# Two score buffers, masks half a row ahead and packed adjacency in a two-layer graph kernel

## The chip, the cores and the metric

The kernel runs on one core of one Trainium2 chip. The metric is the time of one execution on the device in microseconds (us); for a program on one core that is the time of this core. TensorE does the matrix products and the transposes, ScalarE the exponentials and many copies out of PSUM, VectorE the masks, maxima and sums, GpSimd (POOL in the profile) elementwise work on SBUF, and SyncE's queue issues the loads and stores.

## The reference

Inputs are `x` (4096 x 128), a sparse 0/1 matrix `adj` (4096 x 4096, on average 4 ones in a row), two scalars and `weights` (128 x 128), all float32.

```python
deg = clip(adj.sum(axis=1), 1.0);  dis = deg ** (-0.5)
diffusion = (dis[:, None] * adj * dis[None, :]) @ x - x
norms = maximum(norm(x, axis=-1), 1e-8)
sim  = x @ x.T / (norms[:, None] * norms[None, :])
attn = softmax(beta * sim * adj, axis=1)
L0   = diffusion + sigmoid(alpha) * (attn @ x - x)
x1   = layernorm(x + L0)
out  = layernorm(x1 + relu(adj @ (x1 @ weights)))
```

The softmax runs over all 4096 columns of a row: where `adj` is 0 the score is 0, not minus infinity. So the attention is dense, and each block of 128 rows needs 4096 cosines, 4096 exponentials and a product with all of `x`.

## The kernel before

The 4096 rows are 32 row blocks of 128. A row of `r` below is such a block. There are three stages, and inside each the order of every engine's instructions is written out by hand; engines meet only at semaphores (`wait_ge` on a count, `then_inc`).

**Attention stage.** A row is done in 8 steps `h`, each over 512 columns (one PSUM bank). The work on one row, in the order of its data:

1. `land_piece` (SyncE queue, L230) loads a quarter of the row of `adj`, 512 KB, into one of two landing buffers `land`. `cast` (ScalarE, L369) makes bytes of it in `adj_bytes[q]`, with another power of two for each quarter, and sums degrees. `pack` (GpSimd, L287 to L293) adds the four quarters' bytes into one quarter as many words, `packed`. `turn_adj` (TensorE, L838) transposes these into the bank `ps_at`, and `store_adj` (VectorE, L581) unpacks them with a shift and a mask, four operations a row, into `adjT`, which keeps the whole transposed adjacency in SBUF.
2. `cosines` (TensorE, L853): three matmuls (float16 high and low parts) give 128 x 512 cosines in one of two banks `ps_s`. They wait until the mask two groups earlier has read the bank.
3. `mask` (VectorE, L593) multiplies them by the adjacency bytes, writes the buffer `scores` and takes the maximum of the piece. There is one `scores` of 4096 columns. So `mask` of row r+1, step h, waits for `e_turned`: the transposes of row r, step h, have read the same place.
4. `row_max` (VectorE, L602 and L604), behind the last mask, gives the row's maximum. `exps` (ScalarE, L401) are four pieces of 1024 columns in place, with their sums.
5. `turn_e` (TensorE, L864): four transposes of 128 x 128 into one of four banks `ps_e`. `e_high` (ScalarE, L408) and `e_low` (VectorE, L608) copy them as float16 high and low parts to `eT_parts`, four deep.
6. `attend` (TensorE, L877 and L879): four pairs of matmuls add the step's part of the attention to the one accumulator bank `ps_acc`. It runs `LAG = 3` steps behind `turn_e`.
7. `attn_add` (VectorE, L615 and L618), after all eight `attend` of a row, scales `ps_acc` by 1 / sum and adds it to `u`.

Two waits tie this together at the accumulator:

```python
# TensorE, attend(r, h)
pe.wait_ge(e_lo, r * H + (h + 1))
if h == 0 and not start:
    pe.wait_ge(attn_read, r)             # attn_add of rows 0 .. r-1 done
# VectorE, attn_add(r)
dve.wait_ge(attn_part, r * H + H)        # all attend of row r done
```

TensorE's step of row r is: `turn_e(r, h)`; at h = 2 `turn_adj(r)`; then `attend(r, h - 3)`, or at h = 1 `attend(r-1, 7)`; then `cosines(r+1, h+1)` for h = 1 to 6. After step 7 come `attend(r, 5)`, `attend(r, 6)`, each with a cosine group of row r+2. VectorE's step is: at h = 2 `attn_add(r-1)`; `mask(r+1, h)`; at h = 7 `row_max(r+1)`; `e_low(r, h)`; from h = 4 `store_adj(r, h-4)`; from h = 5 a part of the row's sum. ScalarE does two `exps`, then `e_high(r, h)` with the other two `exps` behind h = 1 and 2 and a `cast` of row r+2 behind four others.

**Layer 0 sums.** For each row 32 matmuls (L918) add 8-bit adjacency tiles times `y` (two float16 parts of `x`, scaled by `dis`) in a bank of `ps_e`. `y` is made by GpSimd (L335, L339) and VectorE (`y_low`, L686) near the end of the attention stage, from a second load of `x` into free buffers (L247). The adjacency tiles of the first four rows are read straight from `adjT`; for the others `stage_block` (VectorE, L682) copies a row of `adjT` into one of two stage buffers. Behind the sums VectorE adds (L725, L728) and normalises; TensorE, ScalarE and VectorE make `x1 @ weights` four rows behind (L924, L929, L464, L756).

**Layer 1 sums.** The same with `x1 @ weights` instead of `y`, then relu, add, normalise (L735 to L750), and the store.

Of the kernel before, what the change touches and what calls it, by code (L numbers as in the profile page):

```python
# [26 lines left out]
ALU = mybir.AluOpType  # L27
# [23 lines left out]
def two_layer_gnn(nc, x, adj, alpha, beta, weights, out):  # L51
# [12 lines left out]
    with ExitStack() as ctx:  # L64
# [10 lines left out]
        adjT = sb("adjT", [P, R, B, P], U32)  # L75
        land = sb("land", [P, 2, CH], F32)
# [4 lines left out]
        scores = sb("scores", [P, N], F32)  # L81
# [3 lines left out]
        col = sb("col", [P, 29], F32)  # L85
        packed = sb("packed", [P, CH // K], U32)
# [5 lines left out]
        cmax = sb("cmax", [P, H], F32)  # L92
        csum = sb("csum", [P, C], F32)
# [6 lines left out]
        neg_max, total, r_total, gain = (c(n) for n in range(6, 10))  # L100
# [18 lines left out]
        land_full = [sem("land_full0"), sem("land_full1")]  # L119
        x_again = [sem(f"x_again{q}") for q in range(C)]  # L120
# [72 lines left out]
        x_again_at = ([land[:, q, :].rearrange("p (r d) -> p r d", d=D) for q in range(2)]  # L193
                      + [adj_bytes[:, q, :].bitcast(F32).rearrange("p (r d) -> p r d", d=D) for q in range(2)])
        y_parts = xn_parts[:, :, :].rearrange("p a (r d) -> p r a d", d=D)
        x1t = scores[:, 0:2 * P].rearrange("p (a d) -> p a d", d=P)
        x1_now = scores[:, 2 * P:6 * P].rearrange("p (a d) -> p a d", d=P)
        wts = scores[:, 6 * P:7 * P]
        summed = scores[:, 7 * P:9 * P].rearrange("p (a d) -> p a d", d=P)
# [6 lines left out]
        packed_f = packed[:, :].bitcast(F32)  # L206
        stage = [adj_bytes[:, q, :].bitcast(U32) for q in range(2)]
        stage8 = [adj_bytes[:, q, :].bitcast(F8).rearrange("p (b i k) -> p b i k", b=B, k=K) for q in range(2)]
        adjT8 = [adjT[:, r, :, :].rearrange("p b i -> p (b i)").bitcast(F8)
                 .rearrange("p (b i k) -> p b i k", b=B, k=K) for r in range(G)]  # L210
        adjT_rows = adjT[:, :, :, :].rearrange("p r b i -> p r (b i)")
# [8 lines left out]
        def _(sp):  # L220
            sp.dma_start(u_b[:, 0:2, :], x_v[:, 0:2, :]).then_inc(x_loaded[0], 16)
            sp.dma_start(alpha_c, alpha.rearrange("(a o) -> a o", o=1).to_broadcast([P, 1])).then_inc(small_loaded, 16)
            sp.dma_start(beta_c, beta.rearrange("(a o) -> a o", o=1).to_broadcast([P, 1])).then_inc(small_loaded, 16)
            for q in range(1, C):
                sp.dma_start(u_b[:, 2 * q:2 * q + 2, :], x_v[:, 2 * q:2 * q + 2, :]).then_inc(x_loaded[q], 16)
            sp.dma_start(wts_early, weights).then_inc(w_loaded, 16)

            def land_piece(b, k, i):

                sp.dma_start(land[:, i % 2, :], adj_v[b, k, :, i * CH:(i + 1) * CH]).then_inc(land_full[i % 2], 16)  # L230
# [779 lines left out]
```

## Time and profile before

| | before |
|---|---|
| median of 3 runs | 761.27 us (760.44 to 761.53) |
| span of the profiled execution, first to last instruction | 757.8 us |
| TensorE busy | 721.4 us (95% of the span) |
| VectorE busy | 572.1 us (75%) |
| ScalarE busy | 494.4 us (65%) |
| GpSimd busy | 128.7 us (17%) |
| read from HBM | 71.44 MB |
| attention stage ends (first matmul of layer 0) | 518.0 us |
| layer 0 sums end, layer 1 sums begin | 639.1 us |

The profiler takes one execution; for it the table gives the span on the engines, and the runs' times, taken without a profile, lie 3.5 us above that span in the median. A busy share is an average over stages with different limits, and a busy TensorE is not one at its peak: its matmuls overlap, so durations add up to more than the time they hold the engine. For work on TensorE the distance from start to start is the number to read. On VectorE too an operation's successor can start some 0.07 us before its recorded end.

### The profile page before, as it was taken

Reading aid. Unit: us, or ns where it says so; the run is one execution under the profiler, and the core shown is the slowest. Engines: PE = TensorE matmul, PEld = TensorE weight load, DVE = VectorE, ACT = ScalarE, POOL = GpSimd, SP = SyncE. Lnnn points to the kernel's source line nnn. Section 1 sums busy time; section 2 is a strip of 40 time slices with the busy share of each in tenths; the row PEclk is TensorE's granted clock in tenths of the full one; section 3 lists DMA queues with packets and bytes.
Section 4 is the critical chain, followed back from the end, with each engine's and each line's share of the span. In section 5 each row is a group of like instructions: output and inputs, shape, how many; then the busy total and the mean of one; then the engine's idle time right before and its main releaser. Section 6 shows DMA issues by size and latency. Waiting matters only on the chain. (4 is left out here: it accounts for less than half of the span.)

```text
span 757.8 us, 19379 instructions
## 1 busy us (share of the span) xinstructions
PE 721.4 (95%) x6163; PEld 578.5 (76%) x6163; DVE 572.1 (75%) x1644; ACT 494.4 (65%) x1001; POOL 128.7 (17%) x161
## 2 busy tenths in 40 slices
PE   6889989999999999999999999989999999999997
PEld 6567767777777777777777777768999998888886
DVE  4878878887888788878887888797566666465655
ACT  5888899889988998899889988982122223211111
POOL 2781112111211121112111211170000000000000
PEclk9999999999999999999999999999999999999999
DMA  5645543455445534553445345510000000000000
GB/s 177 189 139 143 159 132 124 127 152 160 115 129 151 160 114 131 150 159 115 130 150 159 115 131 149 169 51 5 1 0 0 0 0 0 12 17 14 28 14 28
DMA packets 22502, 73.81 MB, mean 97 GB/s; under 512 B 2640, under 2 KB 3152, under 8 KB 22480
## 3 DMA queue, kind: packets, MB, share of 16 engines
q1 hardware_dynamic: 22480, 73.54, 32.5%
q8 instruction: 11, 0.18, 0.1%
q14 instruction: 11, 0.09, 0.0%
HBM read 71.44 MB, written 2.10 MB: 97 GB/s over the span
## 5 line engine op out<-in xcount | busy, mean ns | idle before, releaser
L593 DVE CUSTOM_DVE_ANT_1 scores<-ps_s,adj_bytes 128x512 f32<-128x512 f32 x252 | 172.5, 685 | 72.7 <-PE ps_e L864 67.8
L853 PE MATMUL ps_s<-xn_parts,xn_signed 128*128 128x512 f16 x756 | 204.4, 380 | 1.7 <-DVE cmax L593 1.7
L877 PE MATMUL ps_acc<-x_parts,eT_parts 128*128 128x256 f16 x1024 | 192.8, 272 | 4.6 <-DVE u L618 2.0
L879 PE MATMUL ps_acc<-x_parts,eT_parts 128*128 128x128 f16 x1024 | 180.9, 219 | 0.0
L608 DVE SCALAR_TENSOR_TENSOR eT_parts<-ps_e,eT_parts 128x512 f16<-128x512 f32 x256 | 175.2, 685 | 3.7 <-ACT eT_parts L408 3.1
L864 PEld LDWEIGHTS ps_e<-ident,scores 128*128 128x128 f32 x1024 | 123.0, 141 | 69.7 <-issue 27.6
L408 ACT ACTIVATE eT_parts<-ps_e 128x512 f16<-128x512 f32 x256 | 147.0, 587 | 37.3 <-PE ps_e L864 36.6
L864 PE MATMUL ps_e<-ident,scores 128*128 128x128 f32 x1024 | 150.1, 274 | 18.4 <-ACT scores L401 18.4
L401 ACT ACTIVATE scores<-scores,col 128x1024 f32<-128x1024 f32 x128 | 157.6, 1231 | 1.1 <-DVE col L604 1.1
L369 ACT ACTIVATE adj_bytes<-land 128x1024 uint8<-128x1024 f32 x128 | 135.2, 1057 | 23.3 <-DMA land<-in_adj 22.7
L877 PEld LDWEIGHTS ps_acc<-x_parts,eT_parts 128*128 128x128 f16 x1024 | 100.0, 98 | 24.0 <-issue 9.6
L918 PE MATMUL ps_e<-xn_parts,adj_bytes 128*128 128x256 f16 x896 | 105.4, 273 | 0.0
L879 PEld LDWEIGHTS ps_acc<-x_parts,eT_parts 128*128 128x128 f16 x1024 | 100.1, 98 | 5.3
L918 PE MATMUL ps_e<-x_parts,adj_bytes 128*128 128x256 f16 x896 | 98.0, 273 | 0.0
L918 PEld LDWEIGHTS ps_e<-x_parts,adj_bytes 128*128 128x128 fp8e4 x896 | 87.7, 98 | 10.1
L918 PEld LDWEIGHTS ps_e<-xn_parts,adj_bytes 128*128 128x128 fp8e4 x896 | 87.7, 98 | 9.5
L853 PEld LDWEIGHTS ps_s<-xn_parts,xn_signed 128*128 128x128 f16 x756 | 60.2, 98 | 42.5 <-issue 2.1
L287 POOL TENSOR_TENSOR packed<-adj_bytes 128x256 uint32<-128x256 uint32 x32 | 23.3, 728 | 357.9 <-PE ps_at L838 357.9
L453 ACT ACTIVATE col<-mv,col 128x1 f32<-128x1 f32 x64 | 18.6, 291 | 97.7 <-DVE mv L721 97.7
L682 DVE COPY adj_bytes<-adjT 128x1024 uint32 (+1 forms) x56 | 38.8, 693 | 50.2 <-PE ps_e L918 50.2
L487 ACT ACTIVATE scores<-ps_e,col 128x128 f32<-128x128 f32 x32 | 11.8, 369 | 88.9 <-PE ps_e L918 88.9
L581 DVE TENSOR_SCALAR adjT<-ps_at 128x256 uint32 (+1 forms) x128 | 52.6, 413 | 0.0
(113 smaller groups left out, 570.1 us busy)
## 6 DMA issues: line engine op xcount, KB each, us to landing
land<-in_adj SPq DMA_DIRECT2D x128, 512.0 KB, 3.6
u<-in_x SPq DMA_DIRECT2D x4, 512.0 KB, 8.0
out<-u SPq DMA_DIRECT2D x7, 256.0 KB, 2.0
land<-in_x SPq DMA_DIRECT2D x2, 512.0 KB, 3.3
adj_bytes<-in_x SPq DMA_DIRECT2D x2, 512.0 KB, 3.8
out<-u SPq DMA_DIRECT2D x1, 192.0 KB, 1.9
eT_parts<-in_L_gnn_weights SPq DMA_DIRECT2D x1, 64.0 KB, 9.0
scores<-in_L_gnn_weights SPq DMA_DIRECT2D x1, 64.0 KB, 1.7
```

The costliest lines, as they stand in the source:

```text
L369: nc.scalar.activation(adj_bytes[:, q, i * CH:(i + 1) * CH], land[:, i % 2, :], ACT.Copy, scale=float(BYTE_ONE >> i), accum_out=deg[:, i, ...
L401: nc.scalar.activation(scores[:, i * CH:(i + 1) * CH], scores[:, i * CH:(i + 1) * CH], ACT.Exp, bias=neg_max, scale=abs_beta, accum_out=cs ...
L408: nc.scalar.activation(eT_parts[:, h % 4, 0, :], ps_e[:, h % 4, :], ACT.Copy, scale=E_SCALE).then_inc(e_hi, 1)
L581: nc.vector.tensor_scalar(adjT_rows[:, r, i * CH // K:(i + 1) * CH // K], ps_at[:, 0:CH // K].bitcast(U32), i, BYTE_ONE * 0x01010101, ALU. ...
L593: nc.vector.tensor_tensor_reduce(scores[:, o:o + BANK].rearrange("p (k q) -> p k q", k=K), score_bank(h, start).rearrange("p (k q) -> p k ...
L608: nc.vector.scalar_tensor_tensor(eT_parts[:, h % 4, 1, :], ps_e[:, h % 4, :], E_SCALE, eT_parts[:, h % 4, 0, :], ALU.mult, ALU.subtract).t ...
L682: nc.vector.tensor_copy(stage[q], adjT_rows[:, r, :]).then_inc(staged, 1)
L853: ins = nc.tensor.matmul(score_bank(h, start), xn_signed[:, q, part, :], xn_parts[:, other, o:o + BANK], start=(part == 0 and other == 0), ...
L864: ins = nc.tensor.transpose(ps_e[:, h % 4, n * P:(n + 1) * P], scores[:, t * P:(t + 1) * P], ident[:, :])
L877: nc.tensor.matmul(ps_acc[:, 0:2 * D], eT_parts[:, h % 4, 0, n * P:(n + 1) * P], x_parts[:, t, :], start=(t == 0), stop=(t == R - 1), skip ...
L879: ins = nc.tensor.matmul(ps_acc[:, 0:D], eT_parts[:, h % 4, 1, n * P:(n + 1) * P], x_parts[:, t, 0:D], start=False, stop=(t == R - 1), ski ...
L918: return nc.tensor.matmul(ps_e[:, n, 0:2 * D], lhs[:, b, :, k], y[t], start=(t == 0), stop=(t == R - 1))
```

## The change

- **Two score buffers.** `scores` becomes two buffers, one for even and one for odd rows, and `cmax`, `csum`, `neg_max` become two each. `mask` of row r waits for the transposes of row r-2 instead of r-1.
- **Masks and cosines half a row ahead.** In row r, steps 0 to 3 do cosine groups and masks 4 to 7 of row r+1, steps 4 to 7 do groups 0 to 3 of row r+2. `row_max(r+1)` comes in step 3. The prologue does four groups of row 1 instead of two.
- **TensorE's order.** In each step: `turn_e`, at h = 2 `turn_adj`, then `attend` (in steps 0, 1, 2 groups 5, 6, 7 of the previous row), then the cosines. Nothing is left behind step 7.
- **ScalarE's order.** `e_high` and a cast in steps 0 to 3, `e_high` and a piece of the next row's exponentials in steps 4 to 7. In the prologue all exponentials of row 0 and two casts come before the first `e_high`.
- **VectorE's order.** `attn_add(r-1)` moves to step 3. `y_low` moves to steps 4 to 7 of row 31.
- **Packed adjacency.** `store_adj` is one copy of the packed words to `packT`, a quarter of `adjT`'s size. The unpacking moves to `stage_block`: four shift-and-mask operations a row, for all rows of both layers, into one of four stage buffers. Those of rows 0 to 3 of layer 0 are done between the steps of row 31.
- **Buffers.** `land` has four quarters instead of two. `x` is kept in `x_keep`, so the second load of `x` goes. `packed` has two buffers.

```diff
-        adjT = sb("adjT", [P, R, B, P], U32)
-        land = sb("land", [P, 2, CH], F32)
+        packT = sb("packT", [P, R, CH // K], U32)
+        stage = sb("stage", [P, G, N // K], U32)
+        land = sb("land", [P, C, CH], F32)
+        x_keep = sb("x_keep", [P, R, D], F32)
-        scores = sb("scores", [P, N], F32)
+        scores = sb("scores", [P, 2, N], F32)
...
 # SyncE
-                        sp.wait_ge(cast_done, b * (K * C) + (k * C + i - 1))
+                        sp.wait_ge(cast_done, b * (K * C) + ((k - 1) * C + i + 1))
...
 # GpSimd
-                    pool.wait_ge(adj_turned, r)
+                    pool.wait_ge(adj_turned, r - 1)
...
             pool.wait_ge(dis_done, 1)
+            pool.wait_ge(s_done, R * H)
             for q in range(C):
-                pool.wait_ge(x_again[q], 16)
-                y_q = x_again_at[q]
+                y_q = x_keep[:, q * TC:(q + 1) * TC, :]
...
 # ScalarE
             def row(r, q, start=False):
-                casts = (4, 5, 6, 7) if start else (3, 4, 6, 7)
-                exps(r, 0)
-                exps(r, 1)
-                for h in range(H):
-                    if start and h == 2:
-                        cast(1, 1, 3, first=True)
+                for h in range(C):
                     e_high(r, h, start)
...
+                    cast(r + 2, q, h)
+                for h in range(C, H):
+                    e_high(r, h, start)
+                    exps(r + 1, 1 - q, h - C)
+
+            exps(0, 0, 0)
+            cast(1, 1, 2, first=True)
+            exps(0, 0, 1)
+            exps(0, 0, 2)
+            cast(1, 1, 3, first=True)
+            exps(0, 0, 3)
...
 # VectorE
+            def store_adj(r):
+
+                dve.wait_ge(adj_turned, r + 1)
+                nc.vector.tensor_copy(packT[:, r, :], ps_at[:, 0:CH // K].bitcast(U32)).then_inc(adj_stored, 1)
...
                 if not start:
-                    dve.wait_ge(e_turned, r * H + (h + 1 - H))
+                    dve.wait_ge(e_turned, r * H + (h + 1 - 2 * H))
...
-                    if h == 2 and not start:
+                    if h == 3 and not start:
                         if second:
                             dve.wait_ge(u_init, C)
                         attn_add(r - 1)
-                    mask(r + 1, 1 - q, h)
-                    if h == H - 1:
-                        row_max(r + 1)
+                    if h < C:
+                        mask(r + 1, 1 - q, h + C, start)
+                    elif not degrees:
+                        mask(r + 2, q, h - C)
+                    if h == C - 1:
+                        row_max(r + 1, 1 - q)
                     e_low(r, h)
-                    if h >= 4:
-                        store_adj(r, h - 4)
+                    if h == C:
+                        store_adj(r)
                     if h >= 5:
...
-                nc.vector.tensor_copy(stage[q], adjT_rows[:, r, :]).then_inc(staged, 1)
+            def stage_block(k, r, n):
+                for i in range(C):
+                    nc.vector.tensor_scalar(stage[:, n, i * CH // K:(i + 1) * CH // K], packT[:, r, :], i,
+                                            BYTE_ONE * 0x01010101, ALU.logical_shift_left,
+                                            ALU.bitwise_and).then_inc(staged, 1)
...
 # VectorE, row 31
             for h in range(H):
-                if h == 2:
+                if h == 3:
                     attn_add(R - 2)
...
                 e_low(R - 1, h)
...
+                if h < C:
+                    stage_block(h, h, h)
+                if h >= C:
+                    y_low(h - C)
+                if h == C:
+                    store_adj(R - 1)
...
 # VectorE, layers
-                if lag >= G and more:
-                    stage_block(r + 2, n % 2)
+                stage_block(r + G, ahead, n)
                 head0(r, n)
...
 # TensorE
                 for h in range(H):
-                    turn_e(r, h, start)
+                    turn_e(r, q, h, start)
                     if h == 2:
-                        turn_adj(r, start)
+                        turn_adj(r, q, start)
                     if h >= LAG:
                         attend(r, h - LAG, start)
-                    elif h == 1 and not start:
-                        attend(r - 1, H - 1)
-                    if left and 1 <= h < H - 1:
-                        cosines(r + 1, 1 - q, h + 1)
-                for h in range(H - LAG, H - 1):
-                    attend(r, h, start)
-                    if left > 1:
-                        cosines(r + 2, q, h - (H - LAG))
+                    elif not start:
+                        attend(r - 1, h + H - LAG, second)
+                    if h < C and left >= 1:
+                        cosines(r + 1, 1 - q, h + C)
+                    elif h >= C and left >= 2:
+                        cosines(r + 2, q, h - C)
...
-                pe.wait_ge(staged, r + (layer * (R - G) - G + 1))
+                pe.wait_ge(staged, r * C + (layer * R * C + C))
```

## Rows read from the trace of the kernel before

**Rows 1.** The page, busy time by engine: us (share of span) x instructions.

```profile
PE 721.4 (95%) x6163; PEld 578.5 (76%) x6163; DVE 572.1 (75%) x1644; ACT 494.4 (65%) x1001; POOL 128.7 (17%) x161
```

**Rows 2.** Busy time by stretch: us, engines, clock, DMA; rows 30-31, layer 0.

```profile
490.86:518.01 27.15, 23.60 (x222) 19.62 (x223) 25.14 (x58) 21.41 (x36) 15.69 (x11) 1.00 0.18 60
518.01:639.11 121.10, 121.10 (x1111) 109.50 (x1109) 77.19 (x247) 27.10 (x114) 0.00 (x0) 1.00 0.00 0
```

**Rows 3.** Timeline of TensorE, one row block: start, us, line, xcount [idle before].

```profile
218.13 1.09 PE L864 MATMUL ps_e<-ident,scores 128*128 128x128 f32 x8 [0.43 <-ACT scores L401]
...
221.10 0.82 PE L853 MATMUL ps_s<-xn_parts,xn_signed 128*128 128x512 f16 x3
221.75 0.60 PE L864 MATMUL ps_e<-ident,scores 128*128 128x128 f32 x4
222.43 0.27 PE L877 MATMUL ps_acc<-x_parts,eT_parts 128*128 128x256 f16 x1
...
223.09 0.81 PE L853 MATMUL ps_s<-xn_parts,xn_signed 128*128 128x512 f16 x3
...
233.28 0.98 PE L864 MATMUL ps_e<-ident,scores 128*128 128x128 f32 x7 [0.44 <-ACT scores L401]
```

**Rows 4.** Timeline of VectorE in the same row block.

```profile
219.03 0.69 DVE L593 CUSTOM_DVE_ANT_1 scores<-ps_s,adj_bytes 128x512 f32<-128x512 f32 x1 [2.17 <-PE ps_e L864]
...
220.35 0.68 DVE L593 CUSTOM_DVE_ANT_1 scores<-ps_s,adj_bytes 128x512 f32<-128x512 f32 x1
...
220.96 0.68 DVE L608 SCALAR_TENSOR_TENSOR eT_parts<-ps_e,eT_parts 128x512 f16<-128x512 f32 x1
221.56 0.34 DVE L615 SCALAR_TENSOR_TENSOR u<-ps_acc,col,u 128x128 f32 x1
221.93 0.35 DVE L618 SCALAR_TENSOR_TENSOR u<-ps_acc,col,u 128x128 f32 x1
```

**Rows 5.** Timeline of ScalarE in the same row block.

```profile
221.31 0.58 ACT L408 ACTIVATE eT_parts<-ps_e 128x512 f16<-128x512 f32 x1
221.79 1.24 ACT L401 ACTIVATE scores<-scores,col 128x1024 f32<-128x1024 f32 x1
...
223.02 0.58 ACT L408 ACTIVATE eT_parts<-ps_e 128x512 f16<-128x512 f32 x1
...
224.53 0.59 ACT L408 ACTIVATE eT_parts<-ps_e 128x512 f16<-128x512 f32 x1
```

**Rows 6.** Timeline of row 31, VectorE and then TensorE.

```profile
509.96 0.35 DVE L618 SCALAR_TENSOR_TENSOR u<-ps_acc,col,u 128x128 f32<-128x128 f32 x1
...
510.46 0.27 PE L877 MATMUL ps_acc<-x_parts,eT_parts 128*128 128x256 f16 x1 [0.91 <-DVE u L618]
```

**Rows 7.** Groups of instructions by line: busy us, mean ns, idle before.

```profile
L581 DVE TENSOR_SCALAR adjT<-ps_at 128x256 uint32 (+1 forms) x128 | 52.6, 413 | 0.0
L682 DVE COPY adj_bytes<-adjT 128x1024 uint32 (+1 forms) x56 | 38.8, 693 | 50.2 <-PE ps_e L918 50.2
...
L686 DVE TENSOR_TENSOR xn_parts<-land,xn_parts 128x1024 f16<-128x1024 f32 x2 | 3.4, 1684 | 0.0
```

**Rows 8.** Timeline between the layers, VectorE and then TensorE.

```profile
639.09 0.35 DVE L725 SCALAR_TENSOR_TENSOR u<-ps_e,dis_out,u 128x128 f32<-128x128 f32 x1 [1.12 <-PE ps_e L918]
...
641.51 0.49 PE L929 MATMUL ps_acc<-scores 128*128 128x128 f32 x2 [0.27 <-ACT scores L460]
```

**Rows 9.** Timelines of the start: ScalarE, then TensorE twice.

```profile
31.75 1.24 ACT L401 ACTIVATE scores<-scores,col 128x1024 f32<-128x1024 f32 x1 [0.31 <-DVE col L604]
...
13.93 3.62 PE L819 MATMUL ps_e<-ident,scores 128*128 128x128 f32 x16 [4.08 <-DVE scores L534]
...
49.83 1.09 PE L864 MATMUL ps_e<-ident,scores 128*128 128x128 f32 x8 [2.13 <-ACT scores L401]
```

**Rows 10.** Busy time by stretch around the two gaps; the clock is third from last.

```profile
12.00:20.00 8.00, 5.21 (x31) 4.87 (x32) 6.79 (x15) 6.61 (x27) 4.73 (x3) 0.79 0.38 124
...
45.00:53.00 8.00, 5.87 (x50) 4.15 (x48) 4.50 (x15) 7.12 (x13) 6.54 (x8) 1.00 0.59 190
```

More of the change, by code:

```diff
@@ L118, in two_layer_gnn @@
         w_loaded = sem("w_loaded")
[L119 to L120 removed]
+        land_full = [sem(f"land_full{i}") for i in range(C)]
         ident_zero = sem("ident_zero")
@@ L205, in two_layer_gnn @@
         words = [adj_bytes[:, q, :].bitcast(U32).rearrange("p (i w) -> p i w", i=C) for q in range(2)]
[L206 to L211, printed above, removed]
+        packed_f = [packed[:, q, :].bitcast(F32) for q in range(2)]
+        stage8 = [stage[:, n, :].bitcast(F8).rearrange("p (b i k) -> p b i k", b=B, k=K) for n in range(G)]
         def score_bank(h, start):
@@ L394, in _, with exps, e_high @@
             cast(1, 1, 1, first=True)
[L395 to L397 removed]
+            def exps(r, q, i):
                 if i == 0:
                     act.wait_ge(max_done, r + 1)
[L401 to L404 removed]
+                piece = scores[:, q, i * CH:(i + 1) * CH]
+                nc.scalar.activation(piece, piece, ACT.Exp, bias=neg_max[q], scale=abs_beta,
+                                     accum_out=csum[:, q, i:i + 1]).then_inc(exp_done, 1)
+            def e_high(r, h, start=False):
                 act.wait_ge(e_turned, r * H + (h + 1))
@@ L447, in _ @@
                 row(r + 1, 1)
-            late_row(R - 2, 0)
-            late_row(R - 1, 1)
+            e_high(R - 2, 0)
+            e_high(R - 2, 1)
+            e_high(R - 2, 2)
+            act.wait_ge(deg_done, 1)
+            nc.scalar.activation(dis[:, :], dis[:, :], ACT.Sqrt).then_inc(deg_root, 1)
+            e_high(R - 2, 3)
+            nc.scalar.activation(table_loads[1], eps_c, ACT.Exp)
+            for h in range(C, H):
+                e_high(R - 2, h)
+                exps(R - 1, 1, h - C)
+            for h in range(H):
+                e_high(R - 1, h)
+                if h == 0:
+                    nc.scalar.activation(table_loads[2], eps_c, ACT.Sqrt)
             def root(r, q, base):
@@ L648, in _ @@
                                          ALU.mult, ALU.mult))
+            for h in range(C):
+                mask(1, 1, h, start=True)
             def row(r, q, start=False, second=False, degrees=False):
@@ L904, in _ @@
                 cosines(0, 0, h, start=True)
-            cosines(1, 1, 0)
-            cosines(1, 1, 1)
+            for h in range(C):
+                cosines(1, 1, h)
             row(0, 0, start=True)
-            row(1, 1)
+            row(1, 1, second=True)
             with pe.Fori(2, R - 3, 2) as r:
@@ L913, in _ @@
             row(R - 1, 1, left=0)
-            attend(R - 1, H - 1)
+            for h in range(H - LAG, H):
+                attend(R - 1, h)
             def add_tile(n, lhs, t, y):
```

201 lines of the change are left out of this document (77 added, 124 removed).

## The prediction

> **What bounds the kernel now.** I read the page first: TensorE is busy in 95% of the span [rows 1], so I went on to the cut by stage and there to the timeline of one row block [rows 2, 3]. The attention stage, 32 row blocks one after the other, ends at 518 us, two thirds of the span. In the first of the two later stages (sums over the adjacency) TensorE is busy 121.10 of 121.10 us, and the change leaves those matmuls as they are. So what matters is the period of a row block: 15.15 us, from 218.13 to 233.28 in the timeline of one [rows 3].
>
> TensorE's own work in one block, from start-to-start distances in the same rows: four transposes are 0.60 us, of which the last takes 0.27, so 0.11 each, 32 of them 3.52 and the two of the adjacency 0.22; four pairs of attention matmuls 0.66 (222.43 to 223.09), eight times 5.28; a cosine group 0.65 (221.10 to 221.75), eight times 5.2. Sum 14.2 us. The other 0.95 us of the 15.15 is waiting. Most of it lies at the head of the block, where the transposes wait for the exponentials [rows 3]: with one score buffer the masks of the next row can only follow the transposes, so the row's maximum, and the exponentials behind it, come late. About 0.24 us of it is another wait, and it is the one this prediction turns on: `attend(r, 0)` starts at 222.43, though the transposes in front of it started at 221.75 and hold TensorE for 0.44. It waits until VectorE has taken the previous row's sum out of `ps_acc` (`attn_add`, L615 and L618): L618 starts at 221.93, lasts 0.35 and ends at 222.28, and the matmul follows 0.15 later [rows 3, 4]. In row 31 the same wait is plain: the matmul at 510.46 has stood 0.91 us for L618 [rows 6]. So before the change this wait is just about covered, with nothing to spare.
>
> **What the steady row loses.** With two score buffers and masks half a row ahead, the maximum of row r+1 is known at step 3 of row r. Its exponentials run in steps 4 to 7, ahead of the transposes that need them, so the wait at the head of the block goes. ScalarE's step with an exponential piece takes 1.71 us and one with a cast 1.51 (221.31, 223.02, 224.53) [rows 5], TensorE's step is 0.44 + 0.66 + 0.65 = 1.75. ScalarE needs 12.9 us in a block and fits under it, barely in the second half. Four landing buffers give each load almost a block to arrive. VectorE loses three of four unpacking operations of 0.33 a row. None of that is on the path any more, so by themselves these edits would bring the block to 14.2 us, 28 us less over the stage.
>
> **What the steady row gains.** `attn_add(r-1)` moves from step 2 to step 3 of VectorE's row. The last attention group of row r-1 moves from TensorE's step 1 to its step 2, and `attend(r, 0)` stays in step 3. Before, two cosine groups and two of transposes lay between the two; now one of each does. More than that: VectorE's step 2 is `mask(r+1, 6)`, then `e_low(r, 2)`, and `attn_add(r-1)` is queued behind both. `mask(r+1, 6)` needs the cosine group 6, which TensorE issues last in its own step 2. In the kernel before the mask of a step used the cosines of the step before. So the chain from the start of that cosine group is: group 0.82 (its x3 row at 221.10 [rows 3]); start of the mask 0.30 later; mask to `e_low` 0.61 (220.35 to 220.96); `e_low` 0.60 (to 221.56); L615 to L618 0.37; L618 0.35 [rows 4]; to the matmul 0.15 (509.96 + 0.35 to 510.46) [rows 6]. Sum 3.20 us. TensorE is ready for `attend(r, 0)` after 0.65 + 0.44 = 1.09. **Stall: 2.1 us in every block from row 1 on.** Queued behind it on TensorE is cosine group 7, and for that wait `mask(r+1, 7)`, the maximum and the exponentials, but these have a whole half block in hand: from the end of the stall ScalarE's four steps of 1.71 run beside four of 1.75 and are caught up at the next head. I find no second wait.
>
> The 0.30 is the least sure term. The trace has the mask waiting for transposes: those of step 0 end by 218.13 + 0.60, the mask starts at 219.03 [rows 4]. A wait for cosines is not in it. The bounds: 0.03, as L725 starts after its last matmul [rows 8], and 0.45, half as much again as the 0.30, since one more wait instruction stands behind the one that blocks. I take 0.30, the same instruction's own row. The stall is then between 1.85 and 2.25.
>
> The block becomes 14.2 + 2.1 = 16.3 us. Rows 1 to 29 took from 49.83 [rows 9] to 490.86, 441.0 us; they will take 29 x 16.31 = 473.0. **Plus 32** (24 to 36 over the bounds).
>
> **The ends.** *Start:* ScalarE begins the exponentials of row 0 at 31.75 [rows 9] and now does all four (1.23 each, 221.79 to 223.02) and two casts (1.51 less 0.48 for the `e_high`) before the first `e_high` [rows 5], to about 38.8. `attend(0, 0)` then starts near 40.1, and with 0.66 + 0.65 and four steps of 1.75 row 1 starts near 48.5, against 49.83, where TensorE had stood 2.13 us. Two cosine groups more and two attention groups less are done by then, which about cancel (1.30 against 1.32). **Minus 1.2** (0 to minus 2.4).
>
> *Rows 30 and 31* took 27.15 us to the first matmul of the next stage [rows 2]. Now, from the start of row 30: four steps 7.2 with the longer stall of this row 2.4, then 0.6 to the next `e_high` and 0.9 until the maximum is there (mask 7, then L602 and L604), four ScalarE steps with exponentials 6.8, and the first piece of row 31: 18.0. From there VectorE is the bound, because four new unpackings of four operations are put between the pieces of row 31: eight `e_low` 4.8, sixteen operations of 0.335 (0.413 less what overlaps) 5.4, three of the four `y_low` at 1.21 3.6, one copy 0.33, one `attn_add` 0.75, small ones 0.4: 15.3, then 0.8 for the last attention group. Sum 34.1, **plus 7.0**. `y_low` can be longer while GpSimd runs beside it; the mean of the two from `land` is 1.68 [rows 7], which makes 1.5 more, 2.8 if all are as its longest.
>
> The sixteen operations read SBUF, where L581 read PSUM; a copy of 1024 such elements from SBUF to SBUF takes 0.693, only 1.7 times what the 256 of L581 take [rows 7]. At that copy's rate an operation would take some 0.2: the lower bound, 2.2 less. I keep 0.335: same operation, same shape. The Trainium skill (VectorE: DVE Perf Modes, "The perf-mode tier table") lets a 32-bit `tensor_scalar` between SBUF tiles run at two elements a cycle and one from PSUM not. The copy's row agrees for a copy; by that rule the sum would be 2.2 us less here and 0.5 less below.
>
> *Later stages:* a row of the first has VectorE busy 77.19 / 32 = 2.4 of its 3.8 us [rows 2]; four operations (1.34) for one copy (0.61) make it 3.1, some 3.4 with the gaps between dependent ones, so it stays hidden behind TensorE; if that cover went, each 0.1 us over would cost 28 x 0.1 = 2.8. At the change of layers the last row's unpacking now stands in front of L725, which starts at 639.09 and from which the chain leads to the matmul at 641.51, where TensorE already stands 0.27 [rows 8]. **Plus 1.3** (0.8 to 1.4).
>
> Sum: 32.0 - 1.2 + 7.0 + 1.3 = +39.1. The span goes from 757.8 to 797; the median of the runs is 3.5 above that span: 761.3 + 39 = **800 us**.
>
> **The rivals.** *The wait does not bind (faster).* The accumulator wait stays as small as it is if `attn_add(r-1)` is through before TensorE wants `ps_acc`. That needs the chain of 3.20 us to be under 1.09; the sides change at a stall of 0.95, which makes the block 15.15 again. For it: 0.24 was all that it cost before. Against: row 31, where a VectorE busy with other work made it a wait of 0.91 [rows 6], and each of the chain's terms has a row. With no stall: 29 x 14.2 = 411.8, ends as above less 2.4: 737 us. Chance 4%; 1% for ending within 0.2%.
>
> *The clock falls.* Each block now has a gap of 2.1 us, row 30 one of 2.4. After a gap of 4.08 us sixteen transposes took 3.62, twice their pitch, with the granted clock at 0.79 over 12 to 20 us, a mean of its two levels 1.2 and 2.4 GHz; around the gap of 2.13 us before 49.83 it was 1.00 [rows 9, 10]. If each block lost as the start did, half of 3.6 us, that is 29 x 1.8 = 52 more: 852 us. Chance 5%. The Trainium skill (TensorE: Matmul & The Clock Gate, "Part 1: The HAM clock gate") has the clock throttled by default and released by activity, so it speaks against a schedule with holes; the start of this trace agrees, the 2.13 us gap bore no such cost.
>
> *Only the steady stall, cheap ends.* Rows 30 and 31 keep near their old time because unpacking runs at 0.2 and ScalarE sets the pace: 793. It is inside the forecast's range.
>
> **How the numbers follow.** The forecast has 90%. Its range: 800 less 8 (stall), 2.7 (unpacking), 1.2 (start) is 788; plus 4, 2.8 (`y_low`), 1.2 is 808. I add some 3 below and 2 above, as the ends were put together from many small terms: 785 to 810. About what a measurement can tell is 0.2%: faster 0.05, same 0.01, slower 0.94.
>
> **What would show it.** After the change: row blocks 16.3 us apart; TensorE waiting for L618 about 29 times 2.1 us; no wait for exponentials at the head of a block and none of ScalarE for landings; the mask waiting for cosines in each first half; VectorE without a gap through row 31; granted clock 1.00. A block of 14 to 15 us would make the prediction wrong, as would a wait of TensorE for L618 of under 1 us.

## The result and the profile after

The changed kernel takes 822.92 us in the median of 4 runs (822.49 to 825.49), the kernel before 760.97 (760.44 to 761.53) beside it: ratio 1.083, interval 1.081 to 1.085. The direction was forecast, the time was not: 800 was predicted, with 785 to 810 as its range. The profiled execution has a span of 820.7 us, 62.9 more than before.

The page of the changed kernel: busy time by engine, TensorE's granted clock in 40 slices, the shares of the chain that ended last, and three groups (busy us, mean ns | idle before).

```profile
PE 736.7 (90%) x6163; PEld 599.3 (73%) x6163; DVE 570.1 (69%) x1748; ACT 497.3 (61%) x1001; POOL 127.1 (15%) x161
...
PEclk9999999999999999999999999997999999999999
...
PE 58%; ACT 16%; issue 12%; DVE 11%; DMA 1%; ACTq 1%; DVEq 1%; SPq 0%
...
L577 DVE CUSTOM_DVE_ANT_1 scores<-ps_s,adj_bytes 128x512 f32<-128x512 f32 x252 | 173.8, 691 | 146.0 <-PE ps_s L839 121.2
L863 PE MATMUL ps_acc<-x_parts,eT_parts 128*128 128x256 f16 x1024 | 205.6, 281 | 69.9 <-DVE u L602 68.4
...
L670 DVE TENSOR_SCALAR stage<-packT 128x256 uint32 (+1 forms) x256 | 61.6, 303 | 44.5 <-PE ps_e L901 44.5
```

The same 6163 matmuls keep TensorE 15.3 us longer busy than before [rows 1], and its share falls from 95% to 90%. Longer busy with the same instructions is a clock, a lower share is waiting: both are there. The wait is one line: `attend` (now L863) for `attn_add` (L602), 68.4 us. Of TensorE waiting for exponentials at the head of a block, 0.43 us a time before [rows 3], nothing is left in the attention rows.

One block in the timelines of TensorE and VectorE of the changed kernel, where [rows 3, 4] stood before. L839 is `cosines`, L850 `turn_e`, L577 `mask`, L592 `e_low`, L599 and L602 `attn_add`:

```profile
239.97 0.81 PE L839 MATMUL ps_s<-xn_parts,xn_signed 128*128 128x512 f16 x3
240.62 0.60 PE L850 MATMUL ps_e<-ident,scores 128*128 128x128 f32 x4
243.19 0.27 PE L863 MATMUL ps_acc<-x_parts,eT_parts 128*128 128x256 f16 x1 [1.97 <-DVE u L602]
...
241.10 0.69 DVE L577 CUSTOM_DVE_ANT_1 scores<-ps_s,adj_bytes 128x512 f32<-128x512 f32 x1 [0.72 <-ACT adj_bytes L360]
...
241.71 0.69 DVE L592 SCALAR_TENSOR_TENSOR eT_parts<-ps_e,eT_parts 128x512 f16<-128x512 f32 x1
242.32 0.34 DVE L599 SCALAR_TENSOR_TENSOR u<-ps_acc,col,u 128x128 f32 x1
242.69 0.35 DVE L602 SCALAR_TENSOR_TENSOR u<-ps_acc,col,u 128x128 f32 x1
```

This is the predicted chain, term by term. Cosine group 6 starts at 239.97 and ends at 240.78, the mask follows 0.32 later, `e_low` 0.61 later, the two adds 0.61 and 0.98 after that, and `attend` at 243.19: 3.22 us from start to start, where 3.20 was worked out. The profile names a cast (L360) as what released the mask; the cosines it reads ended 0.32 before it, and in the page's group the mask's idle time goes to them, 121.2 of 146.0 us. That the cast doesn't hold it is seen in experiment 4: there the profile names the cosines for the same mask, which starts 0.32 behind their end as here.

The changed kernel by stretch: rows 1 to 29; rows 30 and 31; then three blocks, each from one `attend(r, 0)` to the next, and four half microseconds from the middle one. The clock is third from last, and the first figure is the stretch's length.

```profile
47.10:541.98 494.88, 437.31 (x3539) 337.09 (x3538) 348.17 (x932) 394.19 (x701) 86.13 (x123) 0.96 0.37 119
541.98:578.98 37.00, 25.61 (x234) 21.81 (x232) 29.62 (x70) 18.79 (x32) 11.81 (x8) 0.86 0.01 3
...
208.90:225.20 16.30, 14.33 (x122) 11.18 (x123) 11.98 (x32) 13.36 (x24) 2.76 (x4) 1.00 0.39 124
225.22:243.19 17.97, 16.00 (x122) 12.13 (x123) 11.98 (x32) 13.72 (x24) 2.76 (x4) 0.91 0.37 120
243.19:259.49 16.30, 14.33 (x122) 11.18 (x123) 11.98 (x32) 13.36 (x24) 2.75 (x4) 1.00 0.39 127
...
225.50:226.00 0.50, 0.50 (x6) 0.43 (x4) 0.00 (x0) 0.00 (x0) 0.00 (x0) 0.55 0.89 303
226.00:226.50 0.50, 0.50 (x4) 0.26 (x3) 0.00 (x0) 0.00 (x0) 0.00 (x0) 0.50 1.00 410
...
228.50:229.00 0.50, 0.50 (x6) 0.41 (x4) 0.43 (x5) 0.45 (x1) 0.50 (x1) 0.54 0.00 0
229.00:229.50 0.50, 0.50 (x7) 0.36 (x5) 0.50 (x2) 0.50 (x2) 0.42 (x2) 1.00 0.00 0
```

Two of the three blocks are 16.30 us, as predicted, with the clock at 1.00. The middle one has the same instructions and is 1.67 us longer: in the half microsecond that starts 0.3 us behind the end of the gap at 225.22 the clock falls to about 0.50, the lower of its two levels (1.2 against 2.4 GHz), and comes back at 229. Three cosine matmuls that take 0.81 at the full clock take 1.48 there:

```profile
225.22 0.27 PE L863 MATMUL ps_acc<-x_parts,eT_parts 128*128 128x256 f16 x1 [1.97 <-DVE u L602]
...
226.17 1.48 PE L839 MATMUL ps_s<-xn_parts,xn_signed 128*128 128x512 f16 x3
...
229.29 0.81 PE L839 MATMUL ps_s<-xn_parts,xn_signed 128*128 128x512 f16 x3
```

Read in half microseconds, rows 1 to 29 hold 13 such stretches of about 3.4 us, each beginning less than 0.8 us behind the end of a gap of 1.97 to 1.99. There are 28 gaps of that length, in rows 2 to 29; the one of row 1 is 2.33. That explains rows 1 to 29: 29 blocks of 16.305 are 472.8, 13 times 1.67 are 21.7, together 494.5 of the measured 494.88. It does not say why the other 15, just as long, are followed by the full clock.

The end of the stage, timeline of row 31 in the changed kernel: VectorE, then GpSimd's `y` at the same time, then TensorE. L670 is the unpacking in `stage_block`; [rows 6] stood here before.

```profile
560.24 4.72 DVE L670 TENSOR_SCALAR stage<-packT 128x256 uint32<-128x256 uint32 x4
...
565.48 1.20 DVE L670 TENSOR_SCALAR stage<-packT 128x256 uint32<-128x256 uint32 x4
...
567.21 0.88 DVE L670 TENSOR_SCALAR stage<-packT 128x256 uint32<-128x256 uint32 x4
...
568.39 0.35 DVE L602 SCALAR_TENSOR_TENSOR u<-ps_acc,col,u 128x128 f32<-128x128 f32 x1
...
571.84 0.69 DVE L592 SCALAR_TENSOR_TENSOR eT_parts<-ps_e,eT_parts 128x512 f16<-128x512 f32 x1 [1.70 <-ACT eT_parts L399]
...
559.77 1.90 POOL L327 TENSOR_TENSOR x_keep<-x_keep,norm_r 128x1024 f32<-128x1024 f32 x1
561.75 1.17 POOL L330 TENSOR_SCALAR xn_parts<-x_keep 128x1024 f16<-128x1024 f32 x1
562.89 1.92 POOL L327 TENSOR_TENSOR x_keep<-x_keep,norm_r 128x1024 f32<-128x1024 f32 x1
...
568.88 0.37 PE L863 MATMUL ps_acc<-x_parts,eT_parts 128*128 128x256 f16 x1 [9.01 <-DVE u L602]
```

The first four unpackings take 4.72 us beside GpSimd, the third four 0.88. `attn_add(30)` is queued behind three such groups, so TensorE stands 9.01 us where it stood 0.91 [rows 6], and the clock is low around the end of that gap: rows 30 and 31 have it at 0.86 in the mean. Behind the gap VectorE itself waits 1.70 us, for ScalarE's copy of transposes that TensorE makes only after the gap and at the low clock.

### The profile page after: what moved, and what is told of

Same layout as the page of the kernel before. It is cut to its first block, busy times and chain, and to the rows that moved or that the text cites. A ratio compares the mean times of both kernels' runs of the same rounds, so it can differ in the third digit from the quotient of the medians.

```text
span 820.7 us, 19535 instructions
## 1 busy us (share of the span) xinstructions
PE 736.7 (90%) x6163; PEld 599.3 (73%) x6163; DVE 570.1 (69%) x1748; ACT 497.3 (61%) x1001; POOL 127.1 (15%) x161
## 4 chain that ended last, share of the span: by engine, by line
PE 58%; ACT 16%; issue 12%; DVE 11%; DMA 1%; ACTq 1%; DVEq 1%; SPq 0%
PE ps_e L901 27%; PE ps_s L839 11%; PE ps_acc L863 8%; ACT scores L392 7%; PE ps_e L850 6%; ACT adj_bytes L360 6%; PE ps_acc L865 4%; ACT eT_parts L399 3%; DVE eT_parts L592 3%; DVE scores L577 2%; DVE u L602 1%; DVE u L599 1%; DMA x_keep<-in_x 1%; DVE stage L670 1%; PE ps_acc L912 0%
## 5 line engine op out<-in xcount | busy, mean ns | idle before, releaser
L577 DVE CUSTOM_DVE_ANT_1 scores<-ps_s,adj_bytes 128x512 f32<-128x512 f32 x252 | 173.8, 691 | 146.0 <-PE ps_s L839 121.2
L863 PE MATMUL ps_acc<-x_parts,eT_parts 128*128 128x256 f16 x1024 | 205.6, 281 | 69.9 <-DVE u L602 68.4
L839 PE MATMUL ps_s<-xn_parts,xn_signed 128*128 128x512 f16 x756 | 212.4, 392 | 1.9 <-DVE cmax L577 1.9
L865 PE MATMUL ps_acc<-x_parts,eT_parts 128*128 128x128 f16 x1024 | 190.8, 225 | 0.0
L592 DVE SCALAR_TENSOR_TENSOR eT_parts<-ps_e,eT_parts 128x512 f16<-128x512 f32 x256 | 175.3, 685 | 8.5 <-ACT eT_parts L399 8.4
L850 PEld LDWEIGHTS ps_e<-ident,scores 128*128 128x128 f32 x1024 | 132.7, 146 | 51.2 <-issue 6.2
L863 PEld LDWEIGHTS ps_acc<-x_parts,eT_parts 128*128 128x128 f16 x1024 | 103.2, 101 | 88.3 <-DVE eT_parts L592 67.8
L850 PE MATMUL ps_e<-ident,scores 128*128 128x128 f32 x1024 | 160.5, 281 | 0.0
L360 ACT ACTIVATE adj_bytes<-land 128x1024 uint8<-128x1024 f32 x128 | 134.7, 1052 | 0.0
L901 PE MATMUL ps_e<-xn_parts,stage 128*128 128x256 f16 x1024 | 119.4, 273 | 0.3
L901 PE MATMUL ps_e<-x_parts,stage 128*128 128x256 f16 x1024 | 113.0, 273 | 0.0
L901 PEld LDWEIGHTS ps_e<-x_parts,stage 128*128 128x128 fp8e4 x1024 | 100.2, 98 | 11.5
L901 PEld LDWEIGHTS ps_e<-xn_parts,stage 128*128 128x128 fp8e4 x1024 | 99.7, 98 | 12.0 <-issue 1.1
L839 PEld LDWEIGHTS ps_s<-xn_parts,xn_signed 128*128 128x128 f16 x756 | 65.6, 100 | 39.4 <-issue 4.5
L670 DVE TENSOR_SCALAR stage<-packT 128x256 uint32 (+1 forms) x256 | 61.6, 303 | 44.5 <-PE ps_e L901 44.5
L269 POOL TENSOR_TENSOR xn_signed<-xn_parts,col 128x256 f16<-128x256 f32 (+1 forms) x32 | 19.6, 614 | 384.6 <-PE ps_s L839 384.6
L360 ACT ACTIVATION_READ_ACCUMULATOR adj_bytes<-land (+1 forms) x128 | 25.2, 197 | 0.0
```

Source lines behind the costliest of these rows:

```text
L269: nc.gpsimd.tensor_tensor(xn_signed[:, q, :, :], xn_parts[:, :, bass.ds(r * P, P)], sign_beta.unsqueeze(2).to_broadcast([P, 2, P]), ALU.mu ...
L360: nc.scalar.activation(adj_bytes[:, q, i * CH:(i + 1) * CH], land[:, i, :], ACT.Copy, scale=float(BYTE_ONE >> i), accum_out=deg[:, i, bass ...
L577: nc.vector.tensor_tensor_reduce(scores[:, q, o:o + BANK].rearrange("p (k q) -> p k q", k=K), score_bank(h, r == 0 if start else False).re ...
L592: nc.vector.scalar_tensor_tensor(eT_parts[:, h % 4, 1, :], ps_e[:, h % 4, :], E_SCALE, eT_parts[:, h % 4, 0, :], ALU.mult, ALU.subtract).t ...
L670: nc.vector.tensor_scalar(stage[:, n, i * CH // K:(i + 1) * CH // K], packT[:, r, :], i, BYTE_ONE * 0x01010101, ALU.logical_shift_left, AL ...
L839: ins = nc.tensor.matmul(score_bank(h, start), xn_signed[:, q, part, :], xn_parts[:, other, o:o + BANK], start=(part == 0 and other == 0), ...
```

## The experiments

The theory after the result has three parts. The chain through mask, `e_low` and add costs every block 2 us; the gap that it leaves lets the clock fall in some blocks; the unpackings in row 31 are slow beside GpSimd and hold `attn_add(30)` up. The rivals: the new order as such lengthens the block (two score buffers, cosines last), the falling clock has nothing to do with the gap, and VectorE's load in row 31 alone makes the end long. Ratios below are to the kernel before, run beside each; its median there was 759.4 to 759.7 us, against 760.97 beside the changed kernel, so a difference between times of two experiments can be off by about 1 us.

**1. The add back in step 2**, in the rows and in row 31, all else as changed.

```diff
-                    if h == 3 and not start:
+                    if h == 2 and not start:
...
-                if h == 3:
+                if h == 2:
                     attn_add(R - 2)
```

> The changed kernel with attn_add(r-1) back in VectorE's step 2, in front of mask(r+1, 6); nothing else. My theory (the wait for the accumulator is the whole loss of the steady block, and the clock falls only because of the gap that it makes): the chain is now last attention matmul, L599, L602, and ends about when TensorE gets to attend(r, 0). Blocks of 14.2 to 14.5 us with the granted clock at 1.00 from row 1 to 29; 29 x 2.1 and 13 x 1.67 us come back, and some 2 in row 31: 735 us, 731 to 742. Rival A (the masks behind their own cosines cost by themselves, or ScalarE's steps of 1.71 us are the bound): blocks above 14.8 us, time above 755. Rival B (the clock falls for another reason, such as the order of the matmuls): the clock falls in some 13 blocks still, 757 us.

743.17 us, ratio 0.978 (0.976 to 0.980). One digit, changed in two places, takes away 80 us and turns a loss of 8% into a gain of 2%. It is 1 us above the expected range of 731 to 742: 29 x 2.1 = 61 us were to come back from the rows, and 56 did. Its timeline of TensorE around `attend(r, 0)`, then its windows (rows, end of the stage), then its row 31:

```profile
212.20 0.60 PE L850 MATMUL ps_e<-ident,scores 128*128 128x128 f32 x4
212.86 0.27 PE L863 MATMUL ps_acc<-x_parts,eT_parts 128*128 128x256 f16 x1
...
47.00:478.00 431.00, 428.44 (x3658) 335.09 (x3656) 361.81 (x965) 400.09 (x719) 88.99 (x126) 1.00 0.42 137
478.00:500.00 22.00, 13.91 (x124) 11.99 (x123) 19.46 (x37) 9.01 (x16) 9.83 (x7) 0.77 0.01 4
...
482.38 4.73 DVE L670 TENSOR_SCALAR stage<-packT 128x256 uint32<-128x256 uint32 x4
489.64 0.37 PE L863 MATMUL ps_acc<-x_parts,eT_parts 128*128 128x256 f16 x1 [7.61 <-DVE u L602]
```

A block is 14.385 us, `attend` starts 0.66 behind the transposes' start where 0.44 would be their pitch, so about 0.2 of waiting is left, and the clock is 1.00 through all rows. Against the changed kernel: 29 x (16.305 - 14.385) = 55.7 for the stall and 21.7 for the clock, 77 of the 80. The new order as such is no loss. The end mostly stays: 4.73 us for four unpackings, a gap of 7.61 in place of 9.01, and a low clock.

**2. The gap filled with matmuls that nobody reads**, 17 in the first attempt and 8 in the second, ahead of `attend(r, 0)` in rows 1 to 30. The computation is unchanged; the fillers write a free part of `ps_at`.

```diff
+                        if h == LAG and not start and left >= 1:
+                            for _ in range(17):
+                                nc.tensor.matmul(ps_at[:, 2 * P:3 * P], ident[:, :], ident[:, :],
+                                                 start=True, stop=True)
                         attend(r, h - LAG, start)
```

> The changed kernel with 17 extra identity matmuls (0.11 us each) on TensorE in front of attend(r, 0) in rows 1 to 30, into columns 256 to 383 of ps_at that nothing reads. The wait for L602 stays, TensorE works through it. If the gap is what lets the clock fall: granted clock 1.00 in all these blocks, every block 16.3 us, 13 x 1.67 = 22 us come back: 801 us, and that is the prediction's own sum. If the clock falls for another reason: 822 us or more, with blocks of 17.97 still there.

851.43 us (1.121, 1.118 to 1.123). I had priced a filler at the transposes' 0.11 us, and a filler is recorded as two matmuls and holds TensorE 0.22. Seventeen are 3.7 us and overfill the gap, so blocks are 17.97 us; what the run still shows is a clock of 1.00 in all rows.

> As e2 with 8 extra matmuls instead of 17: the wait for L602 ends at the same moment, TensorE's gap in each block is about 1.2 us instead of 2.1. If any gap of the old size class (the kernel before had 1.05) is harmless: clock 1.00, 801 us as e2. If a gap of 1.2 is enough to let the clock fall in some blocks: between 803 and 823.

801.34 us (1.055, 1.052 to 1.058). Eight fillers are 1.76 us, so this one is really the filled gap. Its timeline, and its window over the rows:

```profile
250.29 1.95 PE L878 MATMUL ps_at<-ident 128*128 128x128 f32 x16
252.42 0.27 PE L863 MATMUL ps_acc<-x_parts,eT_parts 128*128 128x256 f16 x1 [0.19 <-DVE u L602]
...
47.50:541.00 493.50, 486.13 (x4178) 393.58 (x4175) 362.88 (x971) 406.07 (x728) 94.52 (x129) 1.00 0.37 120
```

The add comes when it came before, the block is 16.305 us in every row, and only the clock differs: 21.6 us faster than the changed kernel with 240 matmuls more to do. So the falls go when the gap does.

**3. How much gap it takes.** The same with 3, 2 and 1 fillers, which leaves gaps of 1.30, 1.53 and 1.75 us.

> As e4 with 3 extra matmuls; e4's rows show that one takes 0.22 us and not 0.11, so the gap is 2.0 - 0.66 = 1.3 us in each block, while the blocks stay at 16.3. If a gap of 1.3 us leaves the clock alone: 801 us. If it still lets it fall in some blocks: 803 to 823. The theory that the gap's length decides allows both; the theory that the blocks' length or the order does it says 822.

> The same with two such matmuls, 0.44 us, so the gap is 1.53 us. By the theory that a gap must be nearly as long as 2 us: no fall, 801 us. By the other, that anything over 1.3 will do: falls in some blocks, 803 to 823 us. Both with blocks of 16.3 us at the full clock.

> The changed kernel with one idle identity matmul of 0.22 us ahead of attend(r, 0) in rows 1 to 30, so the gap before it is 1.75 us in place of 1.97 and the block stays 16.3 us. The gap's length decides whether the clock falls, and it leaves the clock alone at 1.3 us: if the turning point lies below 1.75, the clock falls in some of the blocks as it does in the changed kernel, about 13 of 29, and the time is near 823 us (803 to 825). If it lies above, the clock stays at 1.00 and the time is 801.

801.15 us (1.054, 1.050 to 1.058), 801.08 (1.055, 1.051 to 1.059) and 801.54 (1.056, 1.052 to 1.060). The run with one filler, timeline and rows:

```profile
248.83 0.39 PE L878 MATMUL ps_at<-ident 128*128 128x128 f32 x2
250.97 0.27 PE L863 MATMUL ps_acc<-x_parts,eT_parts 128*128 128x256 f16 x1 [1.75 <-DVE u L602]
...
47.50:541.00 493.50, 437.80 (x3747) 345.59 (x3744) 363.27 (x969) 405.50 (x727) 94.22 (x129) 1.00 0.37 119
```

Not one fall in any of the three. One matmul of 0.22 us per block, thrown away, is worth 21 us. In the changed kernel 13 of 28 gaps of 1.97 us cost a slow stretch; of the 28 of 1.75, in the same rows, none does. A filler shortens the gap and adds work at once, and these runs do not separate the two. The expectation of one filler says that the gap's length decides. By itself it does not: row 1 of this run has a gap of 2.10 us without a fall, and experiments 5 and 6 have a fall behind 1.91 and none behind 3.16. Of the two cases in the expectation of one filler, it is the one without falls.

**4. Cosines ahead of the attention matmuls** in TensorE's step, the rest as changed. Group 6, and with it the chain, starts 0.65 us earlier, and `attend(r, 0)` is wanted 0.65 later.

```diff
-                    if h >= LAG:
-                        attend(r, h - LAG, start)
-                    elif not start:
-                        attend(r - 1, h + H - LAG, second)
                     if h < C and left >= 1:
                         cosines(r + 1, 1 - q, h + C)
                     elif h >= C and left >= 2:
                         cosines(r + 2, q, h - C)
+                    if h >= LAG:
+                        attend(r, h - LAG, start)
+                    elif not start:
+                        attend(r - 1, h + H - LAG, second)
```

> The changed kernel with the cosine group in front of the attention matmuls in each of TensorE's steps. VectorE's order is unchanged. The mask of step 2 can start 0.66 us sooner, and TensorE has cosine group 7 to do before attend(r, 0): by the chain the wait is 0.44+0.22 to the cosines, 0.82+0.30+0.61+0.60+0.37+0.35+0.15 = 3.86 us from the start of step 2 against 1.97+0.44+0.65 = 3.06 for TensorE: 0.8 us in place of 2.1, blocks of 15.0 us. With a gap that short I expect the clock to stay at 1.00: 822.9 - 29 x 1.3 - 22 = 763 us (757 to 772). If the order on TensorE does not matter: 822.

763.04 us (1.004, 1.002 to 1.006), on the number expected. The wait is cut by twice 0.65 and the clock never falls in the rows. The mask of step 2, then `attend`:

```profile
219.67 0.69 DVE L577 CUSTOM_DVE_ANT_1 scores<-ps_s,adj_bytes 128x512 f32<-128x512 f32 x1 [0.73 <-PE ps_s L839]
...
221.76 0.27 PE L863 MATMUL ps_acc<-x_parts,eT_parts 128*128 128x256 f16 x1 [0.66 <-DVE u L602]
```

The block is 15.05 us. With the first experiment this pins the stall: it is the length of one chain less the work that TensorE has between its ends, and either end can be moved.

**5. The add in step 3 in the kernel before**, that part of the change alone.

```diff
-                    if h == 2 and not start:
+                    if h == 3 and not start:
```

> The kernel before, with one line changed: attn_add(r-1) in VectorE's step 3 in place of step 2 (rows 1 to 30). If the place of attn_add in VectorE's order is the cause by itself, one buffer or two: a mask and an e_low more (1.21 us) stand in front of it, so TensorE waits 0.24 + 1.2 = 1.45 us for L618 in each block, blocks of 16.3 us: 796 us if the clock stays at 1.00, up to 818 if it falls as in the changed kernel. If the wait needs the new orders of TensorE and the cosines: within 2 us of 761.

778.7 us (1.025, 1.021 to 1.028): between the two cases. Two waits of its timeline, 15.67 us apart, then the wait of row 30 and the stretch behind it:

```profile
215.58 0.27 PE L877 MATMUL ps_acc<-x_parts,eT_parts 128*128 128x256 f16 x1 [1.26 <-DVE u L618]
...
231.25 0.27 PE L877 MATMUL ps_acc<-x_parts,eT_parts 128*128 128x256 f16 x1 [1.26 <-DVE u L618]
...
514.25 0.27 PE L877 MATMUL ps_acc<-x_parts,eT_parts 128*128 128x256 f16 x1 [1.91 <-DVE u L618]
...
514.50:517.50 3.00, 3.00 (x15) 2.02 (x13) 1.46 (x6) 0.30 (x2) 1.58 (x1) 0.50 0.00 0
```

There the mask of a step reads the cosines of the step before, so the chain is shorter: the wait is 1.26 us and not 2. And the block grows by only 0.52, since ScalarE catches up in the gap and the 0.43 us at the head of the block [rows 3] goes. 15.67 - 1.26 is 14.41, the block of experiment 1. The clock falls once, behind the 1.91 us of row 30; behind the waits of 1.26 it is 1.00, and so it is behind a gap of 2.95 us at 51.74. So the late add costs 2.5% on its own; in the changed kernel the masks directly behind their cosines lengthen the wait, and the falls of the clock come on top.

**6. Row 31.** From experiment 1, GpSimd's `y` held back until the 16 unpackings are done.

```diff
             pool.wait_ge(s_done, R * H)
+            pool.wait_ge(staged, G * C)
```

> e1_add_in_step2 with GpSimd's making of y held back until all sixteen unpackings of row 31 are done. If the first unpackings are slow (4.73 us for four, 0.89 for the last four) because GpSimd works on SBUF at the same time: all sixteen take 0.22 each, 3.5 us in place of 7.7, and TensorE's wait in row 31 falls by about 4 us; the time itself stays near 743 (741 to 747), since y comes later. If they are slow for another reason (the first use, packT, the table load): the first four take 4.7 us again.

748.63 us (0.985, 0.981 to 0.989), where 741 to 747 was expected. The timelines of VectorE and TensorE:

```profile
482.62 0.89 DVE L671 TENSOR_SCALAR stage<-packT 128x256 uint32<-128x256 uint32 x4
...
492.12 2.91 DVE L677 TENSOR_TENSOR xn_parts<-x_keep,xn_parts 128x1024 f16<-128x1024 f32 x1 [2.50 <-POOL xn_parts L331]
...
486.23 0.27 PE L864 MATMUL ps_acc<-x_parts,eT_parts 128*128 128x256 f16 x1 [3.97 <-DVE u L603]
```

The same instructions take 0.89 for four in place of 4.73 once GpSimd is quiet, so the rival of mere load on VectorE falls, and TensorE's wait shrinks from 7.61 us to 3.97, about the 4 expected. The overlap only moves, though: `y_low` (L677) now runs beside GpSimd and takes 2.91 us, 1.22 in the changed kernel, and the end comes 5 us later. The cause of the slow unpackings is shown, the cure is not this.

From experiment 1 again, with VectorE's row 31 in another order: `attn_add(30)` first, no unpacking until GpSimd is through, three of the four blocks' unpackings behind the last add.

```diff
             for h in range(H):
-                if h == 3:
+                if h == 2:
                     attn_add(R - 2)
                 e_low(R - 1, h)
-                if h < C:
-                    stage_block(h, h, h)
-                if h >= C:
-                    y_low(h - C)
-                if h == C:
-                    store_adj(R - 1)
+                if h == 3:
+                    store_adj(R - 1)
+                    y_low(0)
+                if h == 4:
+                    y_low(1)
+                if h == 5:
+                    stage_block(0, 0, 0)
+                if h == 6:
+                    y_low(2)
...
+            y_low(3)
             attn_add(R - 1)
+            for h in range(1, C):
+                stage_block(h, h, h)
```

> e1_add_in_step2 and, in row 31, attn_add(30) before anything else that VectorE could put in front of it, the unpacking of row 0 of the adjacency behind e_low(31, 5) and those of rows 1 to 3 behind everything that the first matmuls of layer 0 need. If the end of the stage is slow because 7.7 us of unpacking stand in front of attn_add(30): TensorE's wait of 7.6 us in row 31 falls to 1 or 2, the clock stays at 1.00, layer 0 starts some 8 us sooner: 735 us (732 to 738). If GpSimd's making of y sets the end anyway (its chain ends at 488.1 in e1, layer 0 starts at 499.8 there): 740 or more.

738.13 us (0.971, 0.969 to 0.974), the fastest kernel of this study. Its row 31, and its window up to the layers:

```profile
485.03 0.27 PE L869 MATMUL ps_acc<-x_parts,eT_parts 128*128 128x256 f16 x1 [3.16 <-DVE u L602]
...
490.23 0.88 DVE L670 TENSOR_SCALAR stage<-packT 128x256 uint32<-128x256 uint32 x4
...
40.00:500.00 460.00, 452.51 (x3888) 355.51 (x3886) 386.48 (x1027) 415.70 (x747) 105.81 (x138) 1.00 0.41 133
```

The gap in row 31 is 3.16 us, no unpacking is slow, and the clock is 1.00 to the end of the stage, behind this gap too, though it is longer than any in rows 1 to 30 of the changed kernel. I had expected 735, at most 738: the wait of 3.16 and two of 0.64 and 0.96 for `e_low` are left.

## Why the prediction was wrong

- **The accumulator wait as the new bound, 2.1 us a block:** right. The chain is 3.22 us against 3.20 and the block 16.305 against 16.3. The least sure term, 0.30 from the cosines to the mask, measures 0.32. The wait that the profile prints is 1.97, as it starts at the modelled end of the transposes; from start to start it is 3.22 - 1.09 = 2.13.
- **The step that failed: "around the gap of 2.13 us before 49.83 [the clock] was 1.00".** From this one gap I took it that 29 gaps of the same length bear no cost, and gave the falling clock 5%. It fell behind 13 of 29, 1.67 us each, 21.7 us. Without that the time would be 801, as the four runs with 1, 2, 3 and 8 fillers show. My rival priced the right mechanism (1.8 us a fall, against 1.67) but had it in every block or in none; a part of them was the case that came, and neither the 0.79 of the start [rows 10] nor the one harmless gap could exclude it. The Trainium skill (TensorE: Matmul & The Clock Gate, "A second HAM failure mode: psum-queue depth-cycling") tells of TensorE idling briefly and often between groups of matmuls, with the clock going back and forth between its two levels; the trace agrees, in 13 of 29 blocks; from the same page the prediction had taken only that activity releases the clock.
- **Rows 30 and 31, plus 7.0:** the mechanism was right, the size 2.9 short (37.0 us against 34.1). Two terms make it. The sixteen unpackings, 5.4 in the sum, took 7.7: twelve of them were cheaper than 0.335, 0.22 to 0.30, and the first four took 4.72 us for the 1.34 in the sum. And VectorE was to be without a gap through row 31, but it stood 1.70 us for ScalarE behind TensorE's wait of 9.01, a wait that the sum does not have. Against this, the stall of row 30 was 1.78 us and not 2.4. I had allowed for GpSimd beside `y_low`, and not beside the unpackings, which come first. `y_low` took 1.22. The Trainium skill (SBUF — State Buffer, "SBUF: two separate sides") has VectorE and GpSimd share one pair of ports under a lock that blocks the other for a whole instruction; the trace agrees: the longest unpacking runs from 562.99 to 564.96, and the GpSimd instruction beside it from 562.89 to 564.81.
- **Unpacking outside row 31:** median 0.286 us each and 0.20 from start to start in a group of four (three distances and one length are the 0.89), the lower bound of 0.2. VectorE stayed hidden behind TensorE in the layers.
- **The start, minus 1.2:** row 1 starts at 47.10, minus 2.7, a little past the bound of minus 2.4.
- **The layers, plus 1.3:** 241.7 us from the first sum of layer 0 to the end against 239.8, plus 1.9. The wait at the change of layers is 1.08 where it was 0.27 [rows 8]. The remaining 1.1 lies in layer 0: from its first sum to the first of layer 1 it takes 122.25 us against 121.10 [rows 2], for the same 1111 matmuls. What slows them was not traced.

```profile
704.43 0.49 PE L912 MATMUL ps_acc<-scores 128*128 128x128 f32 x2 [1.08 <-ACT scores L447]
```

- **The sum:** -2.7 + 53.9 + 9.85 + 1.9 = 62.9, where it was -1.2 + 32.0 + 7.0 + 1.3 = 39.1. Of the difference of 23.8, the clock is 21.7. That the rest is only 2.1 is partly luck: the start is 1.5 better than its term, the end 2.9 and the layers 0.6 worse.
- **The rival that the wait does not bind, 737 us,** is a kernel that the runs built: experiment 1 is at 743, as a block takes 14.385 there and not 14.2, with about 0.2 of the wait left.

What stays open: which gaps bring a fall. The 13 lie two or three blocks apart, never in neighbouring ones. Length alone does not sort them: there is none behind 2.13 us before the change, 2.33 in row 1 after it, 2.10 with one filler, 2.95 in experiment 5 and 3.16 in the last run, and there is one behind 1.91 in experiment 5. That it also depends on when in time a gap comes, or on the work around it, would fit; no run varies that with the length kept.

## What to carry over

When two instructions on one engine change places, write down the chain from the last thing that the later one waits for to the engine that waits for it, everything queued ahead of it included, and compare it with the work between on the waiting engine; here the result was right to 0.02 us before anything ran. Then ask what the gap itself does: a stall of 2 us that recurs in each block was followed by half the clock in 13 of 28 cases here, one harmless gap of that length proves nothing, and a range must hold the case in which some of them cost a slow stretch. An instruction whose price comes from a quiet stretch should be priced again where GpSimd runs beside it.

## What the runs showed of the hardware

- Gaps of 1.97 us in TensorE's work, one every 16.3 us, or 18.0 with a fall between, were followed by half the clock for about 3.4 us in 13 of 28 cases; gaps of 1.75, 1.53 and 1.30 us, one every 16.3 us, in none of 28 each.
- Single gaps of 2.10 to 3.16 us, in five runs, were followed by the full clock; one of 1.91 us was followed by half, and so was one of 2.92 that began 7 us behind one of 3.97 (GpSimd held back).
- A float32 matmul of the identity, 128 columns, holds TensorE 0.22 us, where a float32 transpose of the same size holds it 0.11.
- Shift-and-mask operations of 128 x 256 words from SBUF to SBUF take 0.20 us from start to start alone, 0.28 each, and up to 1.97 beside GpSimd; a subtraction of 128 x 1024 takes 1.22 alone and 2.91 beside it.
